# Expert blocks by their turn, and batch 0 of the second attention begun among them

## The reference

```
x = x + tanh(g_xattn[0]) * L0_xattn(layernorm(x), ctx, ctx)     # one head, 120 keys
x = x + tanh(g_ffn[0])   * L0_ffn(layernorm(x))                 # mixture of experts
x = x + tanh(g_xattn[1]) * L1_xattn(layernorm(x), ctx, ctx)     # 16 heads of 16, 120 keys
x = x + tanh(g_ffn[1])   * L1_ffn(layernorm(x))                 # 256 x 256, fp8 values

# L0_ffn: 12 experts, 8 with weights, 4 that return x; the best two per token
topk_logits, topk_idx = top_k(x @ gate_w.T + bias, 2);  w = softmax(topk_logits)
out = sum_e w_e * (silu(x @ w1_e.T) @ w2_e.T)  +  w_zero * x    # w1_e 512 x 256
```

## Time and profile before

| | us |
|---|---|
| median of 3 runs | 363.53 (363.45 to 364.09) |
| the profiled execution | 362.98 |
| its span in the profile | 361.1 |
| busy: PE, DVE, ACT, POOL | 335.3, 256.9, 232.1, 156.9 |
| granted TensorE clock, mean | 0.998 of full |

### The profile page before, as it was taken

How to read it: one execution, slowest core, us unless ns; L and a number is a source line. 1 busy time by engine, 2 the same in 40 slices (tenths; PEclk the granted TensorE clock), 3 DMA queues, 4 the chain that set the end, 5 groups by cost and what they waited for, 6 DMA issues and landing times.

```text
span 361.1 us, 8975 instructions
## 1 busy us (share of the span) xinstructions
PE 335.3 (93%) x2905; PEld 265.5 (74%) x2906; DVE 256.9 (71%) x682; ACT 232.1 (64%) x471; POOL 156.9 (43%) x207
## 2 busy tenths in 40 slices
PE   4999988879999999999999998879999999999995
PEld 2778856649999999999999964656667666666774
DVE  2579988976755656545445487967988988786796
ACT  2589976056676666666766433487577777765596
POOL 7098996275655556555565263212033033002000
PEclk9999999999999999999999999999999999999999
DMA  6999973022222222223333115112021000000005
GB/s 183 314 397 422 420 285 117 16 59 57 77 75 73 73 81 80 73 74 73 81 79 73 45 58 178 56 60 60 4 61 60 2 2 2 3 2 3 2 29 203
DMA packets 15338, 36.21 MB, mean 100 GB/s; under 512 B 3526, under 2 KB 6748, under 8 KB 13772
## 3 DMA queue, kind: packets, MB, share of 16 engines
q1 hardware_dynamic: 10508, 24.66, 18.6%
q0 software_dynamic: 3936, 10.48, 10.4%
q10 hardware_dynamic: 864, 0.66, 0.6%
HBM read 22.28 MB, written 13.52 MB: 99 GB/s over the span
## 4 chain that ended last, share of the span: by engine, by line
PE 74%; DVE 11%; ACT 5%; DMA 4%; POOL 2%; issue 2%; ACTq 0%; DVEq 0%
PE two L1976 15%; PE two L1991 14%; PE two L2130 6%; PE two L2010 5%; PE two L2160 4%; PE two L2195 4%; PE two L2116 4%; PE two L2096 3%; PE two L2001 2%; PE two L1845 2%; PE two L2187 2%; DMA bq_sb<-in_bq 2%; PE two L2176 1%; PE two L1825 1%; ACT xT L916 1%
## 5 line engine op out<-in xcount | busy, mean ns | idle before, releaser
L1387 DVE SCALAR_TENSOR_TENSOR gate<-th,two 128x512 f32<-128x512 f32 x39 | 26.8, 688 | 54.3 <-ACT th L865 27.9
L613 POOL DMA_INDIRECT y_d<-y_sb,goal_i x39 | 38.6, 989 | 50.6 <-ACT y_sb L875 50.6
L607 POOL DMA_INDIRECT xg<-xn_d,slot_i x39 | 38.2, 980 | 21.4 <-DVE slot_i L1330 9.1
L1976 PE MATMUL two<-wh,gh 128*128 x156 | 44.1, 282 | 0.1
L1976 PE MATMUL two<-wh,gl 128*128 x156 | 43.8, 281 | 0.0
L1976 PE MATMUL two<-wl,gh 128*128 x156 | 43.8, 280 | 0.0
L632 POOL TENSOR_TENSOR rstd<-var,half 128x2 f32<-128x2 f32 x14 | 9.9, 708 | 76.8 <-DVE var L1463 76.8
L865 ACT ACTIVATE th<-two 128x512 f32<-128x512 f32 x39 | 23.3, 598 | 29.9 <-PE two L1991 28.7
L854 ACT ACTIVATE xq<-xg 128x256 f32<-128x256 f32 x39 | 23.5, 603 | 28.3 <-DMA xg<-xn_d,slot_i 27.8
L1496 DVE TENSOR_REDUCE nm<-two 128x8 f32<-128x960 f32 x32 | 36.1, 1153 | 4.5 <-PE two L2116 4.1
L969 ACT ACTIVATE pT<-two 120x1024 f32<-120x1024 f32 x32 | 31.1, 1038 | 7.0 <-PE two L2130 7.0
(11 more groups left out here) (307 smaller groups left out, 857.3 us busy)
## 6 DMA issues: line engine op xcount, KB each, us to landing
wl<-in_wmoe SPq DMA_DIRECT2D x8, 1024.0 KB, 13.0
y_d<-wh SPq DMA_DIRECT2D x4, 1024.0 KB
yg<-y_d SPq DMA_DIRECT2D x7, 512.0 KB, 3.5
xn_d<-x_sb SPq DMA_DIRECT2D x8, 258.0 KB, 7.5
x_sb<-in_x SPq DMA_DIRECT2D x8, 256.0 KB, 5.8
out_x<-of SPq DMA_DIRECT2D x8, 256.0 KB, 2.0
xg<-xn_d,slot_i POOLq DMA_INDIRECT x39, 2.9
y_d<-y_sb,goal_i POOLq DMA_INDIRECT x39, 2.4
```

Of the source, the lines that this page charges most:

```text
L607: pool.indirect_dma_start(xg[:, n % 2, :], None, xn_d, bass.IndirectOffsetOnAxis(ap=slot_i[:, n:n + 1], axis=0)).then_inc(gathered[n % 2], 16)
L613: pool.indirect_dma_start(y_d, bass.IndirectOffsetOnAxis(ap=goal_i[:, n:n + 1], axis=0), y_sb[:, n % 2, :], None).then_inc(y_stored[n % 2] ...
L1387: dve.scalar_tensor_tensor(gate[:, k, :], th[:], 1.0, bank[2 + k][:], ALU.add, ALU.mult).then_inc(gate_ok, 1)
L1976: ins = pe.matmul(bank[6 + k][:, 0:D], (gl if part == 2 else gh)[:, k, a], (wl if part == 1 else wh)[:, bass.ds(e + (C * FF + c * D), D)], ...
```

## The change

Blocks are numbered by turns: first the first block of every expert (0 to 7), then the second blocks of the experts that have one, then the third and later ones. `ahead` and `first` get a second plane and a ninth column for that, and `place` is put together from four parts. The block table compares with 15 limits instead of 7.

The results of the first 16 blocks are taken as complete for batch 0: SP loads them (`yg0`) when 16 blocks are stored and `wf8` is made, whose work buffers lie where `yg0` does. DVE runs `quantise_wf` at blocks 4 and 5, `combine(0, u)` at blocks 30 and 31, `stats2(0, u)` behind block 32, `spread2(0)` behind block 33. POOL runs `root2(0)` behind the scatter of block 32 and `split_keys(0)` behind that of 36. ACT runs `norm2(0)` ahead of block 34's slot, `copy_xT2(0)` ahead of 36's, `mask_keys(0)` behind 36's, `copy_q(0)` behind 37's. TensorE runs `transpose_x(0)` ahead of y(36), the queries ahead of y(37), and `scores(0, 0)` right behind y(38), ahead of all waits for y's storage. Batch 0 now goes whole, not in halves; its rows and queries use each other's bank. `goal_i` is made ahead of DVE's four `low` operations. SBUF is laid anew: what batch 0 needs lies under the buffers of the routing and the loop, not under the weights.

```diff
@@ SP @@
+            sp.wait_ge(wf8_ok, 1)
+            for k in range(2):
+                sp.wait_ge(y_stored[k], 16 * E_FFN)
+            sp.dma_start(yg0[:].rearrange("p k u n -> p k (u n)"), y_b[0]).then_inc(y_first, 16)
             sp.wait_ge(y_done, BLOCKS)
...
-            for u, sem_of in ((0, y_half), (1, y_here[0])):
-                sp.dma_start(yg[:, 0, :, u, :], y_b[0][:, :, u * D:(u + 1) * D]).then_inc(sem_of, 16)
@@ POOL @@
             for n in range(BLOCKS):
                 if n + AHEAD < BLOCKS:
                     gather(n + AHEAD)
                 scatter(n)
+                if n == BLOCKS - 7:
+                    root2(0)
+                elif n == BLOCKS - 3:
+                    pool.wait_ge(xq_ok, BLOCKS)
+                    split_keys(0)
@@ ACT @@
+            with act.Fori(1, PAIRS - 3) as i:
+                pair(i)
+            norm2(0)
+            pair(PAIRS - 3)
+            copy_xT2(0)
+            slot(PAIRS - 2, 0)
             act.wait_ge(l1_in, 16 * 4)
+            mask_keys(0)
+            slot(PAIRS - 2, 1)
+            copy_q(0)
+            pair(PAIRS - 1)
...
+            copy_max(0)
+            exp_of(0, 0, 0)
+            exp_of(0, 0, 1)
+            exp_of(0, 1, 0)
             norm2(1)
+            mask_keys(1)
+            exp_of(0, 1, 1)
+            copy_xT2(1)
+            copy_q(1)
+            copy_values(0, 0)
+            norm2(2)
@@ DVE, at the start @@
+            dve.tensor_scalar(block0[:], count[:, 0:E_FFN], float(P), None, ALU.mult)
+            dve.tensor_scalar(to_1[:], count[:, 0:E_FFN], -float(P), float(P * (E_FFN - 1)), ALU.mult, ALU.add)
+            for k, lim in enumerate((lim1, lim2)):
+                dve.tensor_scalar(lim[:], count[:, 0:BLOCKS + 4], -float(E_FFN + k), float(P), ALU.add, ALU.mult)
@@ DVE, routing @@
-            then(dve.scalar_tensor_tensor(cmp[:], over(first[:, 1:E_FFN], BLOCKS + 4), 1.0 / P,
...
+            dve.scalar_tensor_tensor(cmp[:, :, 0:E_FFN - 1], over(first[:, 0, 1:E_FFN], n), 0.0, wide(lim1[:], E_FFN - 1),
+                                     ALU.add, ALU.is_le)
+            then(dve.scalar_tensor_tensor(cmp[:, :, E_FFN - 1:E2], over(first[:, 1, 0:E_FFN], n), first[:, 0, E_FFN:E1],
+                                          wide(lim2[:], E_FFN), ALU.add, ALU.is_le))
...
+            then(dve.scalar_tensor_tensor(blk[:], cmp[:, :, E_FFN - 1], -float(E_FFN), blk[:], ALU.mult, ALU.add))
...
+            own.settle()
+            then(dve.tensor_tensor(second[:], second[:], unused[:], ALU.add))
+            dve.wait_ge(slots_kept, 1)
+            dve.tensor_tensor(goal_i[:], slot_i[:], second[:], ALU.add).then_inc(goals_kept, 1)
@@ DVE, from the loop's end @@
+            pair(PAIRS - 6)
+            for u in range(U):
+                slot(PAIRS - 5, u)
+                combine(0, u)
+            slot(PAIRS - 4, 0)
             stats2(0, 0)
+            stats2(0, 1)
+            slot(PAIRS - 4, 1)
+            spread2(0)
+            for i in range(PAIRS - 3, PAIRS):
+                pair(i)
+            low_q(0)
...
+            for u in range(U):
+                for p in range(2):
+                    maxima(0, u, p)
+            split_max(0)
+            for u in range(U):
+                combine(1, u)
+                stats2(1, u)
+            spread2(1)
@@ PE @@
+            pair(PAIRS - 3)
+            transpose_x(0)
+            e = experts(PAIRS - 2)
+            mix(PAIRS - 2, 0, e[0], None)
+            queries(0, 0)
+            queries(0, 1)
+            mix(PAIRS - 2, 1, e[1], None)
+            e = experts(PAIRS - 1)
+            mix(PAIRS - 1, 0, e[0], None)
+            scores(0, 0)
...
-            unread(4, C * D)
-            pe.wait_ge(y_half, 16)
-            unread(2, C * D)
-            pe.wait_ge(dve_half, 1)
-            unread(1, C * D)
...
+            scores(0, 1)
+            unread(2, C * D, 0)
+            pe.wait_ge(sel_ok, 1)
+            scores_by_key(0, 0)
+            transpose_max(0)
+            less_maxima(0, 0)
+            scores_by_key(0, 1)
+            less_maxima(0, 1)
+            transpose_x(1)
+            pe.wait_ge(bo_ok, 1)
+            pe.wait_ge(one2_ok, 1)
+            queries(1, 0)
+            queries(1, 1)
+            values(0, 0, 0)
+            scores(1, 0)
+            values(0, 0, 1)
```

More of the change, by code:

```diff
@@ L174, in build @@
         count = sb("count", [P, P], F32, con)
-        before = sb("before", [P, E_FFN, E_FFN], F32, con)
+        before = sb("before", [P, E_FFN + 1, E_FFN + 1], F32, con)
+        token16 = sb("token16", [P, TILES, 2], F16, con)
+        rows_are = sb("rows_are", [P, P, 2], F16, con)
+        cols_are = sb("cols_are", [P, BLOCKS, 2], F16, con)
+        part = sb("part", [P, 2, E_FFN + 1], F32, con)
+        block0 = sb("block0", [P, E_FFN], F32, con)
+        to_1 = sb("to_1", [P, E_FFN], F32, con)
+        lim1 = sb("lim1", [P, BLOCKS + 4], F32, con)
+        lim2 = sb("lim2", [P, BLOCKS + 4], F32, con)
         token = sb("token", [P, 2 * TILES], F32, con)
@@ L209, in build @@
         rows_up = sb("rows_up", [P, E_FFN], F32, rt)
-        ahead = sb("ahead", [P, E_FFN, E_FFN], F32, rt)
-        first = sb("first", [P, E_FFN], F32, rt)
+        ahead = sb("ahead", [P, 2, E_FFN + 1, E_FFN + 1], F32, rt)
+        first = sb("first", [P, 2, E_FFN + 1], F32, rt)
+        move1 = sb("move1", [P, E_FFN], F32, rt)
+        move2 = sb("move2", [P, E_FFN], F32, rt)
+        over1 = sb("over1", [P, TILES, E_FFN], F32, rt)
+        over2 = sb("over2", [P, TILES, E_FFN], F32, rt)
         place = sb("place", [P, TILES, E_FFN], F32, rt)
@@ L373, in outputs, with rows_bank, query_bank @@
             return {B - 1: bank[6 - 6 * r], B - 2: bank[1]}.get(b, bank[0])
+        def rows_bank(b):
+            return bank[0] if b else bank[1]
+        def query_bank(b):
+            return bank[1] if b else bank[0]
         def projected(b):
@@ L622, in _ @@
             low(27)
-            pool.wait_ge(goals_kept, 1)
-            pool.wait_ge(zeroed, 16 * ZERO_LOADS)
-            for n in range(BLOCKS):
-                if n + AHEAD < BLOCKS:
-                    gather(n + AHEAD)
-                scatter(n)
             def inverse(rstd_t, var_t, less_t, out_sem):
@@ L898, in _ @@
                 pair(i)
-            with act.Fori(1, PAIRS - 3) as i:
-                pair(i)
-            for i in range(PAIRS - 3, PAIRS):
-                pair(i)
             def norm2(b):
@@ L1413, in _ @@
             xl_of(0, 1)
-            own.settle()
-            then(dve.tensor_tensor(second[:], second[:], unused[:], ALU.add))
-            dve.wait_ge(slots_kept, 1)
-            dve.tensor_tensor(goal_i[:], slot_i[:], second[:], ALU.add).then_inc(goals_kept, 1)
             dve.wait_ge(wf_in, 16)
@@ L1428, in _ @@
                     weights(n)
-                else:
-                    scale_of_wf()
-            with dve.Fori(2, B + 2) as i:
+                elif n == 3:
+                    scale_of_wf()
+                else:
+                    quantise_wf(n - 4)
+            with dve.Fori(3, B + 3) as i:
                 pair_xz(i)
-            with dve.Fori(B + 2, PAIRS - 3) as i:
-                pair(i)
-            for i in range(PAIRS - 3, PAIRS):
+            with dve.Fori(B + 3, PAIRS - 6) as i:
                 pair(i)
@@ L2049, in _ @@
                 pair(i)
-            with pe.Fori(3, PAIRS - 3) as i:
-                pair(i)
-            for i in range(PAIRS - 3, PAIRS):
-                pair(i)
             def transpose_x(b):
```

250 lines of the change are left out of this document (97 added, 153 removed).

## The result

The changed kernel takes **369.3 us** (median of 4 runs, 368.2 to 372.0) for 363.8 of the kernel before in the same set: ratio 1.0142, 95% interval 1.0103 to 1.0181. A second set of six gave 1.0158 (1.0109 to 1.0207). The forecast was 363.0, the range 361.0 to 365.8. The profiled execution took 372.0 us, its span 370.2, 9.1 more than before's.

The account below looks back on a forecast made before the run. TensorE bounds the expert loop, DVE the routing before it; behind the loop, scores(1, 0)'s start decides. Front +1.75 and scores(1, 0) 2.3 earlier, stall included, sum to −0.55: 362.4 us profiled, 363.0 median, range 361.0 to 365.8.

Parts of the forecast that it names:

- The front: Routing before the expert loop: more DVE work, partly recovered at second, makes the loop fill 1.75 us later; bounds +1.2, +2.35.
- Inside the loop: Expert loop: quantise_wf and batch 0's DVE pieces fit into DVE's idle 1.5 us a block, so cost nothing.
- The stall at h(38): Loop's end: norm2(0) on ACT waits for its statistic and delays block 38, so TensorE stalls 1.64 us.
- The tail up to scores(0, 0): From h(38), TensorE resuming at 205.57, to batch 0's first scores at 217.2, 9.0 us earlier than before.
- scores(0, 0) to scores(1, 0), 18.9 us: First scores of batch 0 to those of batch 1: 18.9 us against 12.2 before, putting scores(1, 0) at 236.1.
- another step than before: Sign of being wrong: the batches behind scores(1, 0) were taken to keep the old fixed step.
- the rival that I gave 0.17: TensorE's clock falls behind batch 0's last maxima, slowing queries (+1.7), values and scores (+1.5): 364.7 to 366.2 us; chance 0.17.
- No gap is longer than 2.1 us: Argument against the clock falling behind batch 0's last maxima: TensorE's gaps there stay at or under 2.1 us.
- The other support: Before's emptiest stretch behind the start, TensorE busy 2.58 us of 4, stayed at full clock.
- while TensorE makes the scores, until 218.2: Batch 0 on DVE: sel set up during the scores, done at 218.2, then four maxima of 4.51 us.
- aggregate to normalisation: Batch 1's statistics: aggregate at 226.1, normalisation possible at 227.7; 1.62 us taken from before's profile.
- The rival of a lock at the start: GpSimd's subtractions shut out new DVE operations, first attention up to 5 us late: 365 to 368 us; chance 0.06.

Follow-up runs that it names:

- p1_before: Kernel before with the whole routing part of the change (blocks by turn, second and goal_i ahead), old loop end and batches: 365.5 us, ratio 1.0043.
- c_again: c_after run once more, unedited: 361.6 us, ratio 0.9922 to the kernel before.
- g_before: Kernel before with only the sums of second and goal_i moved ahead of the low operations: 363.1 us, ratio 0.9957.
- sg_after: s_after with unread products filling TensorE's waits between batch 0's scores and batch 1's first scores: 365.9 us, ratio 1.0056.
- gn_after: Changed kernel with sg_after's filling, without the product at the start, and norm2(0) one slot later on ACT: 363.7 us, ratio 0.9996.
- a_again: Changed kernel run once more, unedited: 369.3 us, 368.0 to 376.7; its profile is of the longest execution.
- s_after: Changed kernel with one more 256-column product behind TensorE's first warm product: 369.4 us, ratio 1.0158.
- g1_after: Changed kernel with one of four places filled, two unread 512-column products ahead of batch 1's transposes: 368.3 us, ratio 1.0116.
- s_before: Kernel before with one more 256-column product behind TensorE's first warm product: 364.9 us, ratio 1.0021.
- q_before: g_before with ACT's wait for the first expert weight chunk moved behind copy_keys(2) and copy_xT(1): 364.0 us, ratio 0.9979.
- c_after: gn_after with five moves together, reordering ACT, DVE and GpSimd at batch 1, sel made by ACT, slightly less filling: 361.2 us, ratio 0.9915.
- q_after: Changed kernel with ACT's wait for the first expert weight chunk moved behind copy_keys(2) and copy_xT(1): 368.9 us, ratio 1.0116.
- cn_after: c_after without its unread products in the gap, orders of ACT, DVE and GpSimd kept: 366.4 us, ratio 1.0054.

## Why the prediction was wrong, point by point

- **The front, +1.75: right.** `prod` 1.88 later (said: 1.90), slot_i 2.30 (2.35), x(4) 1.54, TensorE's last gap there 0.30 (0.5). The whole part alone makes the kernel before 1.7 us slower, and `second`'s stall is gone as said. The rule of the Trainium skill that I weighed there (SBUF — State Buffer, "Who interferes with whom") agrees with these traces in both halves: `second` took 2.56 us beside two `wl` subtractions of GpSimd, and `red` 0.67 beside one, for 0.68 in the kernel before. `second`'s move alone is worth 0.8 us to the kernel before (0.6 expected).
- **Inside the loop, 0: too little.** From x(4) to x(38) the changed kernel and its variants take 118.7 to 119.7 us, p1_before 118.3, the kernel before and its variants 118.1 to 118.6. Of this 0.2 to 0.6 stand at one block in every profile, beside `quantise_wf`: its two pieces are 1.4 us each in a gap of 1.5 a block, and DVE worked without a break from 102.5 to 109.0 in c_again. The rest are steps of 3.6 to 4.0 for 3.47 us that move from profile to profile; g_before has two of them as well (3.71 and 3.59).
- **The stall at h(38), +1.64: right.** 1.55 in the profile, 1.85 between the profiles of sg_after and gn_after; the medians differ by 2.2, uncertain by 1.4.
- **The tail up to scores(0, 0): right**, 11.65 us behind h(38) for 11.63.
- **scores(0, 0) to scores(1, 0), 18.9 us: the step that failed.** It took 22.6. In its terms: the sum let the queries of batch 1 run in 2.0 us with their latency; they took 3.8, and the first values 1.08 for 0.64, because the granted clock was 0.50. That is 2.3 us against sg_after's 20.3. The sum also took the batches behind scores(1, 0) for unchanged; the first of them took 14.6 us for 13.5 (15.9 in a_again and s_after), again at the low clock. That was one of my signs of being wrong, "another step than before".

  The fall of the clock was the rival that I gave 0.17; its mechanism held: the emptied gap behind the last maxima, which decides as soon as the clock is down when the queries start. "No gap is longer than 2.1 us" was my argument against it. The longest was 2.52, but that is not where it failed: the clock fell in the first half of that wait, and in g1_after ahead of it, behind waits of 0.47 and 1.22 us. The other support, that the kernel before kept full clock in its emptiest stretch, held for the one profile I had; s_before and q_before, whose edits lie far ahead of this place, show the fall in the old order too. The filling takes 3.4 us off, and 4.7 in c_after's order. The rival's own time, 364.7 to 366.2, was still 3 us short of 369.3, by the terms below.
- **Two sizes in the same step.** `sel` "while TensorE makes the scores, until 218.2": its cast took 1.39 us for 0.41 before, and the maxima began 0.9 late. In the kernel before it began just ahead of GpSimd's copy into `vnow`, and the copy was the long one, 0.63 us for 0.40 in later batches; in the change it began while GpSimd was at its scatter, with the memsets behind that, and the cast ended 0.4 us behind the long memset. The Trainium skill (SBUF — State Buffer, "Who interferes with whom") lets a cast take a mode of two ports, in which it and a GpSimd operation shut each other out; this trace agrees, with 1.39 us. And aggregate to normalisation, taken at 1.6, took 2.48: GpSimd's root and product ran at 0.92 and 0.84 beside DVE's work. Together that is 1.75 us, of which the sum's own slack (norm2(1) possible at 227.7, begun at 228.1) hides 0.4. It accounts for the distance from 18.9 to the 20.3 and 20.5 of the filled gap. That these two causes make it up is argued, not shown: no run takes out one alone, and c_after's 17.9 holds other moves too. The cast and the copy before, and the memset in the change:

```profile
216.20 0.41 DVE L1574 CAST sel<-own_head 128x480 fp32r<-128x480 f32 x1
```

```profile
216.24 0.63 POOL L657 COPY vnow<-v 120x256 f32<-120x256 f32 x1
```

```profile
224.73 0.72 POOL L694 MEMSET vnow<- 120x720 f32 x1
```

- **The sum.** It closes in the profiles. After's span is 9.1 us longer than before's, 9.65 more than the −0.55 of the forecast: start 4.15, front −0.2, loop 0.8, x(38) to scores(0, 0) 0.2, scores(0, 0) to scores(1, 0) 3.7, the step behind it 1.1. q_after's profile, 368.4 us and near the median, has no late start: front 0.2, loop 0.9, x(38) to scores(0, 0) 0.3, then 3.7 and 1.0, which makes 6.0 over the forecast of 362.4. So the failed step and the one behind it are 4.7 of the 6: 3.3 for the clock (2.3 and 1.0) and 1.4 that the filled gap still has over 18.9.
- The rival of a lock at the start is refuted (DVE's next operation, `max0`, waited 0.43 us, for TensorE), and the batches kept the old step once the clock was back (13.4 us).

## What to carry to other kernels

When a change takes work, even work that nobody reads, out of an engine's waits, put it back first and judge the change after: here the same reordering was worth +1.5% without its filling, +0.6% with it, and −1% with it and a few small moves. The longest wait is no test of whether the clock holds, and neither is one profile of the old kernel in which it held: look at the mean clock of several executions, and price every TensorE step behind a row of waits at both clocks. Durations of small DVE and GpSimd operations hold only beside the same neighbours.

## What the runs showed of the hardware

- TensorE's granted clock fell to 0.50 behind waits of 1.26 us and less, 0.6 us into one of 2.52; TensorE worked 1.38 and 1.35 us in two stretches of 4. It was back in the stretch from 248 us on, in which TensorE was busy all 4. In cn_after it came back at 236 to 240, and fell again to 0.57 at 240 to 244, where TensorE was busy all 4 us. The same order of work kept it in the profile of the kernel before and lost it in s_before's and q_before's (0.76 and 0.67 at 236 to 240).
- In the first 20 us the granted clock of the profile can read 1.00 while products run at half speed (1.95 us at 17.72 for 0.97 at 20.27): the duration of a repeated product is the better witness there.
- A DVE cast of 480 columns out of a broadcast took 0.41 us where it began ahead of GpSimd's copy, and 1.39 where it began during GpSimd's scatter and memsets; GpSimd's product of 2 columns 0.20 alone and 0.84 beside DVE operations of two inputs; ACT made the same `sel` in 0.60.
- A fall of the clock in the routing (0.86 and 0.71 at 72 to 80 us in p1_before) cost 0 to 0.5 us where it ended by 82 us, and 1.7 in a_again, where it lasted from 78 to 84.
